# One head's product with adj on GpSimd in the attention stage of a graph-attention kernel

## The chip, the cores and the metric

The kernel runs on one core of a Trainium2 chip. A core has TensorE (PE), VectorE (DVE), ScalarE (ACT), GpSimd (POOL) and SyncE (SP), which issues most transfers here. The metric is the device time of one launch in microseconds, as the median of several runs. Before the change it is 981.29 us (3 runs, 978.91 to 981.9).

## The reference

One graph layer with three attention heads, then a mixture-of-experts layer, over N = 3327 nodes with 128 features. What matters here, for each head with weights W and vector a:

```python
hW = h @ W
hp = (adj > 0) @ hW;  hm = (adj < 0) @ hW
e_plus = leaky_relu(concat([hp, hm]) @ a, 0.2)      # one score per node
att = where(adj > 0, e_plus[None, :], NEG_INF)      # e_minus where adj < 0
att = softmax(att, axis=1)
edge_support += (att * adj) @ hW
```

The diagonal of adj is taken out first. Two GRU cells take the sums further, and the experts follow. In the data adj has no negative entries, so the "plain" branches of the kernel run; a flag made on the chip chooses them.

## The kernel before

N is padded to 3328: 26 tiles of 128 nodes (TILES) down the contracted axis, and 7 column chunks (CHUNKS), the first 256 wide and six 512 wide. The work has stages in a fixed order written out by hand, each engine with its own list of instructions, joined by semaphores. The change touches one stage, the attention over the tiles.

In it every score is used relative to its row's top: the weight of column node c and row node r is exp(shift - max(row[r] - score[c], 0)), and the denominators are multiplied in at the end. For chunk c and tile t (n = 26 c + t) these steps follow each other:

- DVE, `distance` (L1371): two tensor_scalar instructions, heads 0 and 1, subtract and maximum, into wexp slot n % 4 (SLOTS = 4). It counts g_y.
- ACT (L880): relu of head 2's distance into the same slot, counted by g_relu; then one exponential over heads 0 and 1 (L884) and one over head 2 (L886), which counts g_e.
- DVE, `product` (L1380): one tensor_tensor over all three heads, wexp slot times the tile of adj from the ring, the same tile for each head, into wadj buffer n % 2. It waits for g_e and for g_mm, with which TensorE gives the buffer back, and counts g_w.
- PE, `sum_heads` (L1906): one matmul for each head, h[t] times wadj, accumulated over the 26 tiles in three PSUM banks. Each is two records in the profile. The last counts g_mm.

DVE makes tile t + 1's distance ahead of tile t's product. `keep(c)` (L1322 to L1330) multiplies the three finished PSUM banks into `heads`, one instruction a head, eight tiles into the next chunk. The first chunk takes its rows from first_rows (shown as node_w), the others from rowbuf (shown as rows). The loops of DVE and ACT are hardware loops (Fori) with four tiles in a body; TensorE's part is written out.

The tiles of adj come through a ring of 18 slots in thirds of a chunk (THIRDS: tiles 0 to 7, 8 to 15, 16 to 25). SP's `load_third` issues the load of a third when the third two before it has been used (g_w), and puts other transfers behind it in its queue: zero fills of sorted_dram, the broadcasts of the rows (stats_dram, counted by k_in), and weights. POOL's only work in the stage is to clear the diagonal block of each tile that the diagonal crosses (`clear_diagonal`, an affine_select, L657), after each load and ahead of DVE; it counts g_clear, for which DVE waits before the first product of a third. In a later stage POOL makes three elementwise instructions per chunk for the first cell, `edge_mixed` (L692 to L694).

Of the kernel before, what the change touches and what calls it, by code (L numbers as in the profile page):

```python
# [26 lines left out]
H = 128  # L27
HEADS = 3
TILES = -(-N // 128)
# [7 lines left out]
SLOT = 8  # L37
ROWS = 3
SLOTS = 4
ALPHA = 0.2  # L40
# [65 lines left out]
class InOrder:  # L106


    def __init__(self, engine, semaphore):
        self.engine, self.semaphore, self.value = engine, semaphore, 0  # L110
# [26 lines left out]
def graph_layer_kernel(nc, x, x_t, adj_rows, adj_cols, diag, ident_in, sum_parts_in, level_at_in,  # L137
# [9 lines left out]
    with ctx:  # L147
# [216 lines left out]
        g_clear, g_relu, g_order_dve = (sem(f"g_{n}") for n in ("clear", "relu", "order_dve"))  # L364
# [101 lines left out]
        def _(sp):  # L466
# [174 lines left out]
        def _(pool):  # L641
# [10 lines left out]
            def clear_diagonal(c, t, tile):  # L652
# [10 lines left out]
            for c in range(NCH):  # L663
                for part, (t0, t1) in enumerate(LOADS):
                    pool.wait_ge(a_in[part] if c > 0 else a_first[part], 16 * max(c, 1))
                    if c == 0 and t1 > MAIN:
                        pool.wait_ge(a_in_tail, 16)
                    for t in range(t0, t1):
                        clear_diagonal(c, t, cols_of(c, t, t + 1).squeeze(1))
                    nc.gpsimd.nop().then_inc(a_clear, 1)  # L670

            for c in range(NCH):
                for third, (t0, t1) in enumerate(THIRDS):
                    at = (3 * c + third) % 2 * SLOT
                    pool.wait_ge(g_in[third], (32 if third == 2 else 16) * (c + 1))
                    for t in range(t0, t1):
                        clear_diagonal(c, t, ring[:, at + t - t0 if t < t0 + SLOT else SLOT + t - t0, :])
                    nc.gpsimd.nop().then_inc(g_clear, 1)  # L678
# [44 lines left out]
        def _(act):  # L723
# [131 lines left out]
            LAST = HEADS - 1  # L855

# [13 lines left out]
            def exponentials_plain():  # L870

                for c, (c0, w) in enumerate(CHUNKS):

                    def tile(t, k):

                        n = TILES * c
                        slot = (n + k) % SLOTS
                        place = wexp[:, slot, LAST, 0:w]
                        act.wait_ge(g_w, t + (n + 1))
                        nc.scalar.activation(place, row_of(c, LAST), ACT.Relu,  # L880
                                             bias=h[:, bass.ds(t, 1), H + SCORES + LAST]).then_inc(g_relu, 1)
                        act.wait_ge(g_y, t + (n + 1))
                        both = wexp[:, slot, 0:LAST, 0:w]
                        nc.scalar.activation(both, both, ACT.Exp, bias=shift[:, 0:1], scale=-1.0)  # L884
                        act.wait_ge(g_relu, t + (n + 1))
                        nc.scalar.activation(place, place, ACT.Exp, bias=shift[:, 0:1], scale=-1.0).then_inc(g_e, 1)  # L886

                    if c < len(k_in):
                        act.wait_ge(k_in[c], 16)
                    if c == 0:  # L890
                        tiles_by_four(act, 0, SLOT, tile)
                        keep_rows()
                        tiles_by_four(act, SLOT, TILES, tile)
                    else:
                        tiles_by_four(act, 0, TILES, tile)
# [137 lines left out]
        def _(dve):  # L1033
# [327 lines left out]
            def products_plain():  # L1361
# [3 lines left out]
                def distance(c, t, k):  # L1365

                    c0, w = CHUNKS[c]
                    n = TILES * c
                    dve.wait_ge(g_w, t + (n + 1))
                    for i in range(HEADS - 1):  # L1370
                        last = nc.vector.tensor_scalar(wexp[:, (n + k) % SLOTS, i, 0:w], row_of(c, i),  # L1371
                                                       h[:, bass.ds(t, 1), H + i], 0.0, ALU.subtract, ALU.max)
                    last.then_inc(g_y, 1)

                def product(c, t, k, place):
                    c0, w = CHUNKS[c]
                    n = TILES * c
                    dve.wait_ge(g_e, t + (n + 1))
                    dve.wait_ge(g_mm, t + (n + 1))
                    nc.vector.tensor_tensor(wadj[:, k % 2, :, 0:w], wexp[:, (n + k) % SLOTS, :, 0:w],  # L1380
                                            ring[:, bass.ds(place, 1), 0:w].broadcast_to([128, HEADS, w]),
                                            ALU.mult).then_inc(g_w, 1)

                dve.wait_ge(k_in[0], 16)
                distance(0, 0, 0)
                for c in range(NCH):
                    for first, end, at in stretches(c):
# [3 lines left out]
                        if end - first < SLOTS:  # L1391
                            for t in range(first, end):
                                if t + 1 < TILES:
                                    distance(c, t + 1, t + 1)
                                elif c + 1 < NCH:
                                    if c + 1 < len(k_in):
                                        dve.wait_ge(k_in[c + 1], 16)
                                    distance(c + 1, 0, 0)
                                product(c, t, t, at + t - first)
                            continue  # L1400
                        with dve.Fori(0, (end - first) // SLOTS) as p:
                            for k in range(SLOTS):
                                distance(c, SLOTS * p + (first + k + 1), k + 1)
                                product(c, SLOTS * p + (first + k), k, SLOTS * p + (at + k))
# [307 lines left out]
        def _(pe):  # L1712
# [178 lines left out]
            def sum_heads(v):  # L1891
                for c, (c0, w) in enumerate(CHUNKS):
# [311 lines left out]
```

## Time and profile before

| | |
|---|---|
| median of 3 runs | 981.29 us |
| profiled execution, its span | 1004.0 us |
| around the span | the page gives nothing more of that execution |
| attention stage, from the first to the last matmul of L1906 | 262.6 to 716.5 us |
| busy in the span | PE 901.2, DVE 694.9, ACT 628.8, POOL 148.5 us |
| L1906, 1092 matmul records | 444.0 us busy |
| L1380, the product | 299.1 us busy |
| L1371, the distances | 137.1 us busy in the 512 wide chunks |

The profiled execution is one launch taken by the hardware profiler. Its times are microseconds from the first instruction. Durations in groups are means of one instruction in nanoseconds. Matmuls overlap each other, so the distance between the starts of weight loads (PEld) says more about TensorE's pace than the duration of a matmul. Most instructions of DVE begin just before the one ahead has ended, so there too the distance of starts is the pace.

### The profile page before, as it was taken

How to read it: one execution, taken by the hardware profiler on the slowest of the kernel's cores; microseconds unless marked ns; L12 is line 12 of the kernel's file. 1: busy time of each engine (PE TensorE's matmuls, PEld its weight loads, DVE VectorE, ACT ScalarE, POOL GpSimd, SP SyncE). 2: the span in 40 equal slices, each digit the busy share in tenths (PEclk: the TensorE clock that was granted, in tenths of full speed). 3: DMA queues.
4: the chain of work that ended last, by engine and by line, in shares of the span. 5: the costliest groups of instructions: out<-in, count | busy, mean ns of one | idle time of the engine just before them, and what ended most of it. 6: DMA issues, size and time to landing. Idle time of an engine off the chain costs nothing.

```text
span 1004.0 us, 10398 instructions
## 1 busy us (share of the span) xinstructions
PE 901.2 (90%) x2770; PEld 458.4 (46%) x2770; DVE 694.9 (69%) x1287; ACT 628.8 (63%) x922; POOL 148.5 (15%) x184
## 2 busy tenths in 40 slices
PE   5999999899799999999999999999998771587787
PEld 5634343466674344444444444444544331376542
DVE  6523333352799899999999999999667785321234
ACT  2345554511799898998998989989433331564531
POOL 0000000000000000010000001010132555256540
PEclk9999999999899999999999999999999895699989
DMA  9877767220089956645445465220300021455523
GB/s 283 305 249 270 261 228 257 71 87 16 10 214 318 328 180 183 145 120 143 121 121 144 118 179 168 84 104 1 119 1 6 27 72 35 133 145 166 154 98 123
DMA packets 100635, 145.26 MB, mean 145 GB/s; under 512 B 11469, under 2 KB 51079, under 8 KB 99559
## 3 DMA queue, kind: packets, MB, share of 16 engines
q1 hardware_dynamic: 97318, 137.90, 45.5%
q0 software_dynamic: 3264, 6.74, 1.9%
q8 instruction: 24, 0.39, 0.2%
q14 instruction: 29, 0.23, 0.1%
HBM read 122.02 MB, written 22.60 MB: 144 GB/s over the span
## 4 chain that ended last, share of the span: by engine, by line
PE 46%; issue 24%; DVE 19%; ACT 4%; DVEq 3%; POOL 2%; another core or an unknown queue 1%; DMA 1%; SPq 0%; ACTq 0%; POOLq 0%
PE psum L1788 15%; DVE work L1371 9%; PE psum L1906 7%; PE psum L1872 4%; DVE big L1380 3%; PE psum L2093 3%; PE psum L2104 2%; PE psum L2063 2%; DVEq L1371 2%; PE psum L1944 1%; PE psum L1945 1%; PE psum L1771 1%; POOL sorted_dram L703 1%; PE psum L1949 1%; PE psum L1727 1%
## 5 line engine op out<-in xcount | busy, mean ns | idle before, releaser
L1906 PE MATMUL psum<-big,h 128*128 128x512 f32 (+1 forms) x1092 | 444.0, 568 | 13.2 <-DVE big L1380 13.0
L1906 PEld LDWEIGHTS psum<-big,h 128*128 128x128 f32 x1092 | 206.1, 191 | 250.2 <-issue 176.3
L1380 DVE TENSOR_TENSOR big<-work,big 128x1536 f32<-128x1536 f32 (+1 forms) x182 | 299.1, 1643 | 8.3 <-ACT work L886 2.5
L884 ACT ACTIVATE work<-work,shift 128x1024 f32<-128x1024 f32 (+1 forms) x182 | 198.3, 1089 | 42.2 <-DVE work L1371 38.9
L1788 PE MATMUL psum<-big,h 128*128 128x512 f32 x312 | 146.3, 611 | 0.0
L1371 DVE TENSOR_SCALAR work<-rows,h 128x512 f32<-128x512 f32 x312 | 137.1, 482 | 2.8 <-POOLq L678 2.8
L886 ACT ACTIVATE work<-work,shift 128x512 f32<-128x512 f32 (+1 forms) x182 | 123.4, 678 | 0.0
L657 POOL TENSOR_SCALAR_AFFINE_SELECT big<-big 128x128 f32<-128x128 f32 x50 | 25.2, 505 | 633.7 <-DMA big<-adj_cols_dram 631.5
L880 ACT ACTIVATE work<-rows,h 128x512 f32<-128x512 f32 x156 | 110.6, 709 | 0.0
L1788 PEld LDWEIGHTS psum<-big,h 128*128 128x128 f32 x312 | 56.6, 191 | 68.9 <-issue 68.4
L756 ACT ACTIVATE work<-big 128x2048 bf16<-128x2048 f32 (+1 forms) x42 | 75.0, 1786 | 11.9 <-POOLq L670 9.3
L1126 DVE TENSOR_SCALAR rows<-big 128x2048 fp8e4<-128x2048 f32 x36 | 42.5, 1224 | 48.9 <-POOLq L670 48.7
L1672 DVE TENSOR_SCALAR rows<-psum,rows 128x128 f32<-128x128 f32 x58 | 17.7, 348 | 76.2 <-PE psum L2114 30.1
L716 POOL DMA_INDIRECT y_dram<-rows x58 | 55.6, 959 | 54.3 <-DVE rows L1663 37.6
L703 POOL DMA_INDIRECT sorted_dram<-big x44 | 43.9, 997 | 33.1 <-issue 12.5
L1113 DVE TENSOR_TENSOR work<-work,psum 32x512 f32<-32x512 f32 (+1 forms) x7 | 4.5, 637 | 54.2 <-ACT work L771 54.2
L2093 PE MATMUL psum<-work,rows 128*128 128x256 f32 x116 | 32.5, 406 | 7.3 <-ACT work L996 5.1
L2104 PE MATMUL psum<-work,rows 128*128 128x256 f32 x116 | 32.4, 404 | 5.7 <-issue 3.4
L1872 PE MATMUL psum<-rows,work 128*126 128x512 fp8e4 (+1 forms) x168 | 35.0, 364 | 0.0
L1005 ACT ACTIVATE work<-psum,rows 128x256 f32<-128x256 f32 x58 | 24.5, 479 | 15.3 <-PE psum L2093 11.4
L771 ACT ACTIVATE work<-psum 32x512 f32<-32x512 f32 (+1 forms) x7 | 3.9, 557 | 39.1 <-PE psum L1749 39.0
L2104 PEld LDWEIGHTS psum<-work,rows 128*128 128x128 f32 x116 | 22.9, 202 | 11.2 <-issue 4.7
(296 smaller groups left out, 832.8 us busy)
## 6 DMA issues: line engine op xcount, KB each, us to landing
big<-adj_cols_dram SPq DMA_DIRECT2D x30, 2048.0 KB, 8.0
sorted_dram<-zeros SPq DMA_DIRECT2D x15, 910.0 KB, 14.3
big<-adj_cols_dram SPq DMA_DIRECT2D x9, 1024.0 KB, 7.3
big<-adj_cols_dram SPq DMA_DIRECT2D x6, 1536.0 KB, 6.5
rows<-experts_dram SPq DMA_DIRECT2D x29, 257.5 KB
rows<-stats_dram SPq DMA_DIRECT2D x1, 4608.0 KB, 27.2
rows<-stats_dram SPq DMA_DIRECT2D x1, 3840.0 KB, 20.4
rows<-sorted_dram SPq DMA_DIRECT2D x29, 130.0 KB
```

The source lines that it names most:

```text
L716: nc.gpsimd.indirect_dma_start(out=y_dram[:, :], out_offset=bass.IndirectOffsetOnAxis(ap=where_i[:, n, k:k + 1], axis=0), in_=y_sb[:, n % ...
L756: nc.scalar.activation(unused[:, 0:t1 - t0, 0:w], cols_of(c, t0, t1), ACT.Relu, scale=-1.0, accum_out=negative[:, NQ * c + g:NQ * c + g + ...
L880: nc.scalar.activation(place, row_of(c, LAST), ACT.Relu, bias=h[:, bass.ds(t, 1), H + SCORES + LAST]).then_inc(g_relu, 1)
L884: nc.scalar.activation(both, both, ACT.Exp, bias=shift[:, 0:1], scale=-1.0)
L886: nc.scalar.activation(place, place, ACT.Exp, bias=shift[:, 0:1], scale=-1.0).then_inc(g_e, 1)
L1371: last = nc.vector.tensor_scalar(wexp[:, (n + k) % SLOTS, i, 0:w], row_of(c, i), h[:, bass.ds(t, 1), H + i], 0.0, ALU.subtract, ALU.max)
L1380: nc.vector.tensor_tensor(wadj[:, k % 2, :, 0:w], wexp[:, (n + k) % SLOTS, :, 0:w], ring[:, bass.ds(place, 1), 0:w].broadcast_to([128, HEA ...
L1788: last = nc.tensor.matmul(bank[2 + c % 2][:, 0:w], h[:, t, 0:H], cols_of(c, t, t + 1).squeeze(1), start=t == 0, stop=t == TILES - 1)
L1872: last = nc.tensor.matmul(bank[6 + c % 2][0:STAT * LH, 0:w], weights[k][:, t - PREP * k, 0:STAT * LH], mask_of(t, c), start=t == 0, stop=t ...
L1906: done = nc.tensor.matmul(sums[i], h[:, t, 0:H], wadj[:, t % 2 if v == "plain" else 0, i, 0:w], start=t == 0, stop=t == TILES - 1)
L2093: last = nc.tensor.matmul(bank[2 + n % 2][:, a * BATCH:(a + 1) * BATCH], w1_of[a][:, n % NX, :], turned[:, n % 3, :], start=True, stop=True)
L2104: last = nc.tensor.matmul(bank[4 + n % 2][:, 0:BATCH], w2_of[a][:, n % NX, :], act_h[:, n % 3, a, :], start=a == 0, stop=a == HALVES - 1)
```

## The change

DVE's product covers heads 0 and 1 (1024 elements wide instead of 1536); POOL makes head 2's with a tensor_tensor of its own and counts g_p. PE, ACT's relu and SP's loads get a wait on g_p. ACT's relu is issued a tile ahead, and one exponential covers all three heads. DVE makes the distances two tiles ahead. POOL clears the diagonal of the next third after tiles 3, 11 and 20 of a chunk, between products, where it had no order with products before. The loops of DVE and ACT are written out. LAST is 2, the third head.

```diff
 (SP, load_third)
                     sp.wait_ge(used, TILES * ((n - 2) // 3) + THIRDS[(n - 2) % 3][1] + credit)
+                    sp.wait_ge(g_p, TILES * ((n - 2) // 3) + THIRDS[(n - 2) % 3][1])
 (POOL)
+            def clear_third(order, n):
+
+                c, third = n // 3, n % 3
+                t0, t1 = THIRDS[third]
+                at = n % 2 * SLOT
+                pool.wait_ge(g_in[third], (32 if third == 2 else 16) * (c + 1))
+                for t in range(t0, t1):
+                    clear_diagonal(order, c, t, ring[:, at + t - t0 if t < t0 + SLOT else SLOT + t - t0, :])
+                nc.gpsimd.nop().then_inc(g_clear, 1)
+
+            def products():
+
+                clear_third(plain_order, 0)
+                for c, (c0, w) in enumerate(CHUNKS):
+                    for t in range(TILES):
+                        n = TILES * c + t
...
+                        pool.wait_ge(g_e, n + 1)
+                        pool.wait_ge(g_mm, n + 1)
+                        nc.gpsimd.tensor_tensor(wadj[:, n % 2, LAST, 0:w], wexp[:, n % SLOTS, LAST, 0:w], ring[:, at, 0:w],
+                                                ALU.mult).then_inc(g_p, 1)
+                        if t in (3, 11, 20) and 3 * c + t // 8 + 1 < 3 * NCH:
+                            clear_third(plain_order, 3 * c + t // 8 + 1)
 (ACT, exponentials_plain)
+                def distance(c, t):
...
+                    if n >= SLOTS:
+                        act.wait_ge(g_p, n - SLOTS + 1)
+                    nc.scalar.activation(wexp[:, n % SLOTS, LAST, 0:w], row_of(c, LAST), ACT.Relu,
+                                         bias=h[:, t:t + 1, H + SCORES + LAST]).then_inc(g_relu, 1)
+
+                distance(0, 0)
                 for c, (c0, w) in enumerate(CHUNKS):
...
+                        act.wait_ge(g_y, n + 1)
+                        act.wait_ge(g_relu, n + 1)
+                        place = wexp[:, n % SLOTS, :, 0:w]
                         nc.scalar.activation(place, place, ACT.Exp, bias=shift[:, 0:1], scale=-1.0).then_inc(g_e, 1)
 (DVE, products_plain)
+                def product(c, t, place):
...
+                    nc.vector.tensor_tensor(wadj[:, n % 2, 0:LAST, 0:w], wexp[:, n % SLOTS, 0:LAST, 0:w],
+                                            ring[:, place:place + 1, 0:w].broadcast_to([128, LAST, w]),
                                             ALU.mult).then_inc(g_w, 1)
...
-                distance(0, 0, 0)
+                distance(0, 0)
+                distance(0, 1)
...
+                        for t in range(first, end):
+                            ahead = TILES * c + t + 2
+                            if ahead < TILES * NCH:
+                                distance(ahead // TILES, ahead % TILES)
+                            product(c, t, at + t - first)
 (PE, sum_heads)
                         pe.wait_ge(g_w, TILES * c + t + 1 + SLOTS)
+                        if v == "plain":
+                            pe.wait_ge(g_p, TILES * c + t + 1)
```

## Rows read from the trace of the kernel before

**Rows 1.** The page: busy time, share of the span and instructions of each engine.

```profile
PE 901.2 (90%) x2770; PEld 458.4 (46%) x2770; DVE 694.9 (69%) x1287; ACT 628.8 (63%) x922; POOL 148.5 (15%) x184
```

**Rows 2.** Busy time by stretch: PE, PEld, DVE, ACT, POOL; then clock, DMA share, GB/s.

```profile
439.50:507.90 68.40, 67.25 (x157) 29.47 (x156) 67.75 (x82) 61.91 (x79) 2.76 (x4) 1.00 0.54 141
```

**Rows 3.** Timeline of DVE, 512 wide chunk: start, us, engine, line.

```profile
480.45 1.76 DVE L1380 TENSOR_TENSOR big<-work,big 128x1536 f32<-128x1536 f32 x1
482.13 0.88 DVE L1371 TENSOR_SCALAR work<-rows,h 128x512 f32<-128x512 f32 x2
483.03 1.76 DVE L1380 TENSOR_TENSOR big<-work,big 128x1536 f32<-128x1536 f32 x1
```

**Rows 4.** Timeline of the weight loads at the end of the stage.

```profile
713.28 0.19 PEld L1906 LDWEIGHTS psum<-big,h 128*128 128x128 f32 x1 [0.24 <-DVE big L1380]
...
715.85 0.19 PEld L1949 LDWEIGHTS psum<-support,big 128*128 128x128 f32 x1 [0.24 <-issue]
```

**Rows 5.** Timeline of SP's queue: the same third of two chunks.

```profile
439.50 0.37 SPq L510 DMA_DIRECT2D big<-adj_cols_dram  x1
...
507.87 0.37 SPq L510 DMA_DIRECT2D big<-adj_cols_dram  x1
```

**Rows 6.** Groups of the span by form: count, busy us, mean ns, idle before.

```profile
L1380 DVE TENSOR_TENSOR big<-work,big 128x1536 f32<-128x1536 f32 x156 | 274.2, 1758 | 5.0 <-issue 1.1 <-PE psum L1906 0.8 <-ACT work L886 0.3
L1380 DVE TENSOR_TENSOR big<-work,big 128x768 f32<-128x768 f32 x26 | 24.9, 956 | 3.3 <-ACT work L886 2.2 <-PE psum L1906 1.1
L1329 DVE TENSOR_TENSOR rows<-rows,psum 128x512 f32<-128x512 f32 x18 | 11.3, 680 | 3.3 <-PE psum L1906 3.3
```

**Rows 7.** Timeline of DVE, first chunk.

```profile
271.13 0.95 DVE L1380 TENSOR_TENSOR big<-work,big 128x768 f32<-128x768 f32 x1
...
272.53 0.95 DVE L1380 TENSOR_TENSOR big<-work,big 128x768 f32<-128x768 f32 x1
```

**Rows 8.** Groups of POOL by form, later stage.

```profile
L694 POOL TENSOR_TENSOR work<-work 128x512 f32<-128x512 f32 x5 | 6.3, 1262 | 0.4
L694 POOL TENSOR_TENSOR work<-work 128x256 f32<-128x256 f32 x1 | 0.7, 725 | 0.1
```

**Rows 9.** Timeline of DVE and POOL, later stage.

```profile
788.31 0.69 DVE L1446 TENSOR_TENSOR work<-work 128x512 f32<-128x512 f32 x1
789.04 1.94 DVE L1447 TENSOR_TENSOR work<-work 128x512 f32<-128x512 f32 x1
789.13 1.28 POOL L692 TENSOR_TENSOR work<-h_t,work 128x512 f32<-128x512 f32 x1
...
790.50 1.61 POOL L693 TENSOR_TENSOR work<-work 128x512 f32<-128x512 f32 x1
```

**Rows 10.** Timeline of DVE and POOL, later stage, small operands.

```profile
760.38 0.21 DVE L1507 TENSOR_TENSOR big<-big 128x48 f32<-128x48 f32 x1
...
766.31 1.27 POOL L693 TENSOR_TENSOR work<-work 128x512 f32<-128x512 f32 x1
766.44 1.20 DVE L1573 TENSOR_TENSOR big<-big 128x48 f32<-128x48 f32 x1
```

**Rows 11.** Timeline, attention stage: a diagonal clearing and a distance.

```profile
450.12 0.36 POOL L657 TENSOR_SCALAR_AFFINE_SELECT big<-big 128x128 f32<-128x128 f32 x1
...
450.25 0.51 DVE L1371 TENSOR_SCALAR work<-rows,h 128x512 f32<-128x512 f32 x1
```

**Rows 12.** DMA issues at 301.17, 321.83 and 439.50: size, us to landing.

```profile
big<-adj_cols_dram SPq DMA_DIRECT2D x1, 2048.0 KB, 18.9
...
big<-adj_cols_dram SPq DMA_DIRECT2D x1, 2048.0 KB, 20.9
...
big<-adj_cols_dram SPq DMA_DIRECT2D x1, 2048.0 KB, 8.4
```

**Rows 13.** PE's busy time by stretch, with the granted clock behind it.

```profile
870.00:880.00 10.00, 8.13 (x43) 1.00 0.29 79
...
910.00:920.00 10.00, 8.23 (x36) 0.83 0.55 158
```

More of the change, by code:

```diff
@@ L39 @@
 SLOTS = 4
+LAST = HEADS - 1
 ALPHA = 0.2
@@ L363, in graph_layer_kernel @@
         g_y, g_e, g_w, g_mm, g_kept = (sem(f"g_{n}") for n in ("y", "e", "w", "mm", "kept"))
-        g_clear, g_relu, g_order_dve = (sem(f"g_{n}") for n in ("clear", "relu", "order_dve"))
+        g_clear, g_relu, g_order_dve, g_p = (sem(f"g_{n}") for n in ("clear", "relu", "order_dve", "p"))
         early_in, t_ready = sem("early_in"), sem("t_ready")
@@ L650, in _, with clear_diagonal @@
                 .then_inc(consts, 1)
-            def clear_diagonal(c, t, tile):
+            def clear_diagonal(order, c, t, tile):
                 c0, w = CHUNKS[c]
@@ L668, in _ @@
                     for t in range(t0, t1):
-                        clear_diagonal(c, t, cols_of(c, t, t + 1).squeeze(1))
+                        clear_diagonal(order, c, t, cols_of(c, t, t + 1).squeeze(1))
                     nc.gpsimd.nop().then_inc(a_clear, 1)
[L672 to L678, printed above, removed]
+            def clear_third(order, n):
[6 more added lines that the diff above has]
+                nc.gpsimd.nop().then_inc(g_clear, 1)
@@ L679, in _ @@
+            plain_order, signed_order = (InOrder(pool, pool_order, order.value) for _ in range(2))
+            pool.wait_ge(f_ready, 1)
+            signed = pool.value_load(flag[0:1, 0:1])
+            with pool.If(signed > 0):
+                nc.gpsimd.nop().then_inc(g_p, TILES * NCH)
+                for n in range(3 * NCH):
+                    clear_third(signed_order, n)
+            with pool.Else():
+                products()
+            order.value = plain_order.value
             pool.wait_ge(sorted_clear, 16 * PARTS)
@@ new lines, in distance @@
+                def distance(c, t):
+                    w = CHUNKS[c][1]
+                    n = TILES * c + t
+                    if t == 0 and c < len(k_in):
+                        act.wait_ge(k_in[c], 16)
+                    if n >= SLOTS:
+                        act.wait_ge(g_p, n - SLOTS + 1)
+                    nc.scalar.activation(wexp[:, n % SLOTS, LAST, 0:w], row_of(c, LAST), ACT.Relu,
+                                         bias=h[:, t:t + 1, H + SCORES + LAST]).then_inc(g_relu, 1)
@@ new lines, in exponentials_plain @@
+                distance(0, 0)
+                for c, (c0, w) in enumerate(CHUNKS):
+                    for t in range(TILES):
+                        n = TILES * c + t
+                        if t + 1 < TILES:
+                            distance(c, t + 1)
+                        elif c + 1 < NCH:
+                            distance(c + 1, 0)
+                        act.wait_ge(g_y, n + 1)
+                        act.wait_ge(g_relu, n + 1)
+                        place = wexp[:, n % SLOTS, :, 0:w]
+                        nc.scalar.activation(place, place, ACT.Exp, bias=shift[:, 0:1], scale=-1.0).then_inc(g_e, 1)
+                        if c == 0 and t == SLOT - 1:
+                            keep_rows()
@@ L1363, in products_plain, with distance @@
                 nc.vector.nop().then_inc(g_w, SLOTS)
[L1365 to L1372, printed above, removed]
-                    last.then_inc(g_y, 1)
[L1375 to L1381, printed above, removed]
+                def distance(c, t):
+                    w = CHUNKS[c][1]
+                    n = TILES * c + t
+                    if t == 0 and c < len(k_in):
+                        dve.wait_ge(k_in[c], 16)
+                    dve.wait_ge(g_w, n + 1)
+                    for i in range(LAST):
+                        last = nc.vector.tensor_scalar(wexp[:, n % SLOTS, i, 0:w], row_of(c, i),
+                                                       h[:, t:t + 1, H + i], 0.0, ALU.subtract, ALU.max)
+                    last.then_inc(g_y, 1)
+                def product(c, t, place):
+                    w = CHUNKS[c][1]
+                    n = TILES * c + t
+                    dve.wait_ge(g_e, n + 1)
+                    dve.wait_ge(g_mm, n + 1)
+                    nc.vector.tensor_tensor(wadj[:, n % 2, 0:LAST, 0:w], wexp[:, n % SLOTS, 0:LAST, 0:w],
+                                            ring[:, place:place + 1, 0:w].broadcast_to([128, LAST, w]),
                                             ALU.mult).then_inc(g_w, 1)
-                dve.wait_ge(k_in[0], 16)
-                distance(0, 0, 0)
+                distance(0, 0)
+                distance(0, 1)
                 for c in range(NCH):
@@ L1390, in products_plain @@
                         dve.wait_ge(g_clear, 3 * c + min(first // SLOT, 2) + 1)
[L1391 to L1404, printed above, removed]
+                        for t in range(first, end):
[3 more added lines that the diff above has]
+                            product(c, t, at + t - first)
                 keep(NCH - 1)
```

26 lines of the change are left out of this document (4 added, 22 removed).

## The prediction, made before the changed kernel was run

> **What bounds the kernel now.** I read the busy shares first [rows 1]: TensorE 90%, VectorE 69%, and GpSimd only 15%, so GpSimd looks like free room. Shares of a span mix stages, so next comes the table by stretch [rows 2]. It shows one column chunk of 26 tiles in the middle of the attention stage, 68.4 us, with PE busy 67.3, DVE 67.8 and ACT 61.9 us of it. Two engines are full at once. The rows of one tile say how full [rows 3]. DVE starts a tile's product at 480.45 and the next at 483.03, 2.57 us apart: the product's successor starts 1.67 us after it (482.13), and the two distances take 0.88, 0.02 from the next start. That is 1.67 + 0.90 = 2.57 with no gap. TensorE, at the end of the stage when all data lie ready, starts its weight loads 0.43 us apart, the six of a tile from 713.28 to 715.85 [rows 4]: also 2.57 us, and the granted clock of the stretch is 1.00 [rows 2]. So DVE and TensorE tie, and any relief of DVE alone is worth nothing inside a tile. What it can give back lies in two places. First, SyncE issues the load of the same third of two successive chunks at 439.50 and 507.87 [rows 5]: 68.37 us per chunk, 1.45 more than 26 x 2.57 = 66.9. That is DVE's keep() between two chunks, three instructions of 0.68 us [rows 6], partly covered. Second, in the first chunk, of half width, DVE's products start 1.40 us apart [rows 7], against 2.57 / 2 = 1.29 for TensorE.
>
> **The change, step by step.** *(1) DVE's product shrinks from 1536 to 1024 elements.* The 1536 and 768 element forms take 1.758 and 0.956 us [rows 6]: 1.044 ns an element, so 512 fewer are 0.53 us. DVE's own tile falls to 2.57 - 0.53 = 2.04 us, and in the first chunk to 1.40 - 0.27 = 1.13.
>
> *(2) ACT.* It is busy 61.9 / 26 = 2.38 us per tile [rows 2] and does the same elements in one instruction fewer, so it stays below the other bounds: worth nothing. The relu moved a tile ahead and the distances moved two tiles ahead take latency out of a chain that holds nobody up now. ACT's relu gets a new wait, for GpSimd's product of four tiles before; behind it stands the exponential of the present tile, but four slots are over 9 us of cover against a product that may take 2.4.
>
> *(3) GpSimd's new product of 512 elements.* The same operation, type and size stands in a later stage: 1.26 us, and 0.73 for 256 [rows 8]. Against 2.57 us a tile it seems to fit easily, and by engine busy times alone the change would be free. But look at what DVE does while such a product runs [rows 9]. DVE's L1447 (two SBUF inputs, 512 elements) takes 1.94 us where the same form one instruction earlier took 0.69. It started at 789.04; GpSimd's L692 ran 789.13 to 790.41; DVE ended 790.98, 0.57 after GpSimd, and its 512 elements need 0.53. So DVE moved nothing until GpSimd was through. The reverse stands there too: GpSimd's next product, started 790.50, took 1.61, and ended 1.13 after DVE's end at 790.98. A second place [rows 10]: a DVE product of 48 elements takes 1.20 us, ending 767.64, with a GpSimd product ending 767.58; its form costs 0.21 [the first of rows 10]. And the distances (one SBUF tensor in) are held as well [rows 11]: with GpSimd's diagonal clearing from 450.12 to 450.48, the distance started 450.25 ends 450.76, which is 450.48 plus 0.28. Its 512 elements take about that if they pass two at a time (0.53 / 2 = 0.27), and its free time is 0.44, half of rows 3's 0.88.
>
> So GpSimd's product and all three DVE instructions of a tile exclude each other, and their times add. What GpSimd adds to DVE's tile: it holds DVE off for 1.13 us, DVE starts some 0.03 after, and DVE's normal step between two instructions (1.67 less 1.60 of elements, 0.07) is covered: 1.13 + 0.03 - 0.07 = 1.09. Where it falls into the wider step between two distances (0.44 less 0.27 of elements = 0.17) it adds 0.99. I take 1.05: **2.04 + 1.05 = 3.09 us per tile**, against 2.57. Bounds: from below, elements alone at GpSimd's slope ((1.262 - 0.725) / 256 = 2.1 ns, so 1.07) with 1.07 and 0.53 of DVE, 2.67, some 2.8 with the steps between them; from above, DVE's measured loss in rows 9, 1.94 - 0.69 = 1.25, so 3.3.
>
> The Trainium skill (SBUF — State Buffer, "Who interferes with whom") calls this an exclusive lock: a DVE instruction with two SBUF inputs, or in a two-port mode, and a GpSimd instruction that reads SBUF block each other for the whole instruction. Rows 9 to 11 agree on who blocks whom. Taken to the letter, with GpSimd's whole 1.26 us added to 2.04, a tile would be 3.30 us and the time 156 x 0.21 = 33 us above my forecast; by rows 9 a part of it (1.26 - 1.13) hides behind the instruction before.
>
> The sum: a chunk is 26 x 3.09 = 80.3 us plus 1.5 for keep(), which reads PSUM for its second input and may let GpSimd's product pass beside it: 81.8, or +13.5 over 68.37. Six chunks: **+81 us**. First chunk: GpSimd's 256 elements add 1.05 - (1.26 - 0.73) = 0.52, so 1.13 + 0.52 = 1.65 against 1.40, 26 times: **+6**. TensorE's 2.57 fits into 3.09, and with two wadj buffers a buffer is back after both products (2.4 in sequence), the matmuls (2.57) and waits of some 0.3: 5.3 us, within two tiles' 6.2. So the buffer loop doesn't bind.
>
> *(4) GpSimd's diagonal clearing now stands in line with products.* clear_third waits for the load of the next third after tiles 3, 11 and 20; behind it is the next tile's product, then TensorE. The load is issued when its ring slots come free, 4 or 5 tiles earlier, 12.4 to 15.5 us at the new pace. In the steady stage 2 MB land in 8.4 us: no cost. Two early ones took 18.9 (issued 301.17) and 20.9 us (321.83) [rows 12], crowded by the broadcasts of stats_dram and the zero fills; until now they were needed 8 tiles after. Now GpSimd would stand 18.9 - 12.4 = 6.5 and 20.9 - 12.4 = 8.5 us; the slower pace thins the crowd, and DVE runs ahead meanwhile, so about half: **+7** (bounds 0 and 15). SyncE's new wait for g_p delays a load by GpSimd's lag, under a tile, and stands before the same zero fills and early weight loads; the slack is above. DVE's wait for k_in comes a tile earlier, with two tiles' products queued behind it; the broadcasts go out before the loads of rows 12, and these are in before the chunk that reads them.
>
> *(5) Loops written out.* Nothing: TensorE's part is already written out and its loads keep their 0.43 pitch [rows 4]; DVE's steps show no loop gap in rows 3 to be won. If code came late, it would show as idle before it; I allow 0 to +5.
>
> Together 81 + 6 + 7 = **+94 us**. The profiled execution's span is 1004.0 us; with it the sum gives 1098. The page has no time around the span, and the median of the runs is 981.29, 22.7 below. The stage runs at full clock with PE and DVE at their own pitch, so nothing in it is stretched by profiling, and I add the +94 to the median: 981.3 + 94 = 1075, and with half a microsecond each for GpSimd's new branch and the stage's last product **1076 us**.
>
> **The rivals.** *No exclusion (the change works).* For it: GpSimd idles 85% of the span, and rows 9 to 11 are few instructions, most on other tiles. Then TensorE binds: a chunk falls to 66.9 (6 x 1.45 = 9 us), the first gives 26 x 0.11 = 3: 969 us. Against it: every overlapped pair in the groups shows the block, in both directions. It turns at one point: GpSimd's product must add less than 0.53 us to DVE's tile, what it takes off; above that the kernel is slower. 5%.
>
> *Partial overlap.* The products alternate so that steps and start-ups hide: 2.8 us per tile, 156 x 0.23 = 36, and 2 each for the first chunk and the loads: +40, 1021 us. Nothing in the rows speaks for it but that the samples are few. 10%.
>
> *Worse: TensorE's clock falls.* At 2.57 of 3.09 us TensorE is 83% busy in bursts. A later stretch with 82% busy shows a granted clock of 0.83 [rows 13], another with 81% one of 1.00. A clock of 0.83 is a third of the time at 1.2 GHz, where a tile takes 5.14: of 480 us, 160 make 31 tiles instead of 52, 21 x 3.09 = 65 us more: 1141 us. Against it: the gaps are 0.5 us, and those of the later stage are longer. 13%, with a GpSimd that queues up behind loads for the full 16 us in the same class.
>
> **How the numbers follow.** Forecast 72%, the rivals 5, 10 and 13. About 0.3% (3 us) is what can be told from no change. Faster: 5%, the first rival. Of the partial case's 10, 2 may land within 0.3%; the rest is slower, 72 + 8 + 13 = 93%. Range: 156 tiles at 2.9 with no load waits give 51 + 4 = +55, 1036; at 3.3 with the load waits 114 + 8 + 12 = +134, 1115. 1040 to 1114 leaves out some 10% on either side.
>
> **What would show it.** In the changed profile GpSimd's product should take over 1.3 us on average, up to 2.3, although free it takes 1.27; where DVE's distances are 0.88 for two now, one of them should often pass 1.3, or its 1024 form the 1.76 - 0.53 = 1.22 that it costs free; the same third's load should be issued some 82 us apart; PE should wait about half a microsecond per tile, ended by whichever product came last. GpSimd should stand on a DMA after tiles 3 and 11 of the second chunk only. I am wrong if DVE's forms keep their free times while GpSimd's product runs, or if chunks are below 75 us; and wrong in size if the clock row leaves 1.00.

## The result, and the profile after

The changed kernel takes 1039.57 us (median of 4 runs, 1037.46 to 1041.93) against 981.19: a ratio of 1.0597, 95% interval 1.0581 to 1.0613. It is 58.4 us slower. The forecast was 94 us slower, 1076, with a range of 1040 to 1114: the side and the mechanism came out, the size was too large by 36 us and the time lies just under the range. One execution of a later run, half_product, took 1148.7 us at a granted clock of 0.79 and is left out of its time.

The page of the changed kernel shows what a busy share hides. The row that answers to [rows 1]:

```profile
PE 935.0 (90%) x2770; PEld 446.4 (43%) x2770; DVE 756.0 (73%) x1287; ACT 598.2 (58%) x740; POOL 398.2 (38%) x366
```

GpSimd took over a third of DVE's product, and DVE's busy time rose by 61 us. The groups by form of the attention stage say where [rows 6]; columns are count, busy us, mean ns, idle before:

```profile
L1402 DVE TENSOR_SCALAR work<-rows,h 128x512 f32<-128x512 f32 x312 | 278.9, 934 | 0.0
L694 POOL TENSOR_TENSOR big<-work,big 128x512 f32<-128x512 f32 x156 | 230.1, 1476 | 225.5 <-PE psum L1931 213.1 <-DMA big<-adj_cols_dram 6.5 <-ACT work L922 5.1
L1412 DVE TENSOR_TENSOR big<-work,big 128x1024 f32<-128x1024 f32 x156 | 197.3, 1265 | 8.3 <-PE psum L1931 8.2
```

The product shrank as worked out (1.22 free, 1.27 on average). But the distances, which the change hardly touches, went from 137.1 us in 312 instructions to 278.9. The timelines of DVE and of GpSimd show one tile; each row is taken from a stretch that cuts the pair of distances apart, since a merged row would hide which of the two is held:

```profile
603.52 1.21 DVE L1412 TENSOR_TENSOR big<-work,big 128x1024 f32<-128x1024 f32 x1
604.66 0.47 DVE L1402 TENSOR_SCALAR work<-rows,h 128x512 f32<-128x512 f32 x1
...
605.05 1.49 DVE L1402 TENSOR_SCALAR work<-rows,h 128x512 f32<-128x512 f32 x1
606.47 1.21 DVE L1412 TENSOR_TENSOR big<-work,big 128x1024 f32<-128x1024 f32 x1
```

```profile
604.83 1.43 POOL L694 TENSOR_TENSOR big<-work,big 128x512 f32<-128x512 f32 x1 [1.52 <-PE psum L1931]
```

GpSimd starts its product at 604.83, when TensorE gives the buffer back, and waits until the first distance ends (604.66 + 0.47 = 605.13). It is through at 606.26, 1.13 us later, the hold read in [rows 9]. The second distance starts at 605.05 and ends at 606.54, 0.28 after GpSimd. So a tile is 1.14 (product to first distance) + 0.39 (first to second distance) + 1.42 (second distance to next product) = 2.95 us, where TensorE needs 2.57 (the median over chunks 3 to 6 is 2.944). The chain of waits of that stretch, in order of time (start, us, what), has nothing else in it; the 1.49 of L1402 is the held distance:

```profile
602.11 1.49 DVE work L1402
603.60 1.13 DVE big L1412
604.73 0.01 DVE work L1402
604.75 0.30 issue
605.05 1.49 DVE work L1402
```

By stretch, the columns as in [rows 2], DVE is never idle and TensorE's rows cover 95% at full clock, though it needs only 2.57 of 2.95 us. SyncE issues the same third 77.59 us apart, where [rows 5] had 68.37:

```profile
470.10:547.70 77.60, 73.76 (x156) 27.49 (x156) 77.60 (x82) 56.89 (x53) 40.01 (x30) 1.00 0.50 124
```

```profile
437.68 0.37 SPq L512 DMA_DIRECT2D big<-adj_cols_dram  x1
...
515.27 0.37 SPq L512 DMA_DIRECT2D big<-adj_cols_dram  x1
```

From the first weight load of each chunk to that of the next, the seven chunks took 41.5, 69.8, 68.4, 68.4, 68.4, 68.5 and 68.2 us before (453.3 in all) and 48.3, 81.8, 77.5, 77.6, 77.7, 77.6 and 76.4 after (516.9). That is 63.6 more; what lies ahead of the stage is the same to 0.2 us.

The profiled span of before (1004.0) can't be set against that of after (1037.4). The kernel before took 981 us on two of the chips used and 1004 and 1007 on two others. What follows the stage took 258 to 260 us in all profiles on the first kind, 282 to 288 on the second; it is 288.1 in the profile of before, so that one is taken to be of the second kind. So times are compared only with the runs of before on the same chip, and chunks, which don't differ by chip from the third on, across all.

### The profile page after: what moved, and what is told of

Same layout as the page of the kernel before. It is cut to its first block, busy times and chain, and to the rows that moved or that the text cites. A ratio compares the mean times of both kernels' runs of the same rounds, so it can differ in the third digit from the quotient of the medians.

```text
span 1037.4 us, 9741 instructions
## 1 busy us (share of the span) xinstructions
PE 935.0 (90%) x2770; PEld 446.4 (43%) x2770; DVE 756.0 (73%) x1287; ACT 598.2 (58%) x740; POOL 398.2 (38%) x366
## 4 chain that ended last, share of the span: by engine, by line
DVE 46%; PE 33%; issue 8%; DMA 5%; POOL 4%; ACT 2%; SPq 2%; DVEq 0%; POOLq 0%; PEld 0%; ACTq 0%
DVE work L1402 21%; DVE big L1412 17%; PE psum L1811 15%; DMA big<-adj_cols_dram 4%; PE psum L1895 4%; PE psum L1931 2%; PE psum L2088 2%; POOL y_dram L746 2%; PE psum L1794 1%; POOL sorted_dram L733 1%; PE psum L1750 1%; PE psum L2165 1%; PE psum L1969 1%; PE psum L1970 1%; PE psum L1974 1%
## 5 line engine op out<-in xcount | busy, mean ns | idle before, releaser
L1931 PE MATMUL psum<-big,h 128*128 128x512 f32 (+1 forms) x1092 | 486.8, 584 | 34.3 <-POOL big L694 12.1
L694 POOL TENSOR_TENSOR big<-work,big 128x512 f32<-128x512 f32 (+1 forms) x182 | 251.8, 1385 | 290.1 <-PE psum L1931 233.9
L922 ACT ACTIVATE work<-work,shift 128x1536 f32<-128x1536 f32 (+1 forms) x182 | 269.9, 1483 | 121.5 <-DVE work L1402 121.4
L1931 PEld LDWEIGHTS psum<-big,h 128*128 128x128 f32 x1092 | 196.6, 193 | 323.7 <-issue 174.0
L1402 DVE TENSOR_SCALAR work<-rows,h 128x512 f32<-128x512 f32 x312 | 278.9, 934 | 0.0
L1412 DVE TENSOR_TENSOR big<-work,big 128x1024 f32<-128x1024 f32 (+1 forms) x182 | 216.1, 1187 | 13.4 <-PE psum L1931 13.2
L1811 PEld LDWEIGHTS psum<-big,h 128*128 128x128 f32 x312 | 56.6, 192 | 68.7 <-issue 68.0
L2118 PE MATMUL psum<-work,rows 128*128 128x256 f32 x116 | 29.9, 381 | 1.9 <-ACT work L1025 1.9
L2129 PE MATMUL psum<-work,rows 128*128 128x256 f32 x116 | 30.0, 381 | 0.0
L1895 PEld LDWEIGHTS psum<-rows,work 128*126 128x126 bf16 x168 | 21.9, 136 | 11.1 <-issue 0.5
```

What stands on the lines that cost most here:

```text
L694: nc.gpsimd.tensor_tensor(wadj[:, n % 2, LAST, 0:w], wexp[:, n % SLOTS, LAST, 0:w], ring[:, at, 0:w], ALU.mult).then_inc(g_p, 1)
L1402: last = nc.vector.tensor_scalar(wexp[:, n % SLOTS, i, 0:w], row_of(c, i), h[:, t:t + 1, H + i], 0.0, ALU.subtract, ALU.max)
L1412: nc.vector.tensor_tensor(wadj[:, n % 2, 0:LAST, 0:w], wexp[:, n % SLOTS, 0:LAST, 0:w], ring[:, place:place + 1, 0:w].broadcast_to([128, L ...
L1811: last = nc.tensor.matmul(bank[2 + c % 2][:, 0:w], h[:, t, 0:H], cols_of(c, t, t + 1).squeeze(1), start=t == 0, stop=t == TILES - 1)
L1895: last = nc.tensor.matmul(bank[6 + c % 2][0:STAT * LH, 0:w], weights[k][:, t - PREP * k, 0:STAT * LH], mask_of(t, c), start=t == 0, stop=t ...
L1931: done = nc.tensor.matmul(sums[i], h[:, t, 0:H], wadj[:, t % 2 if v == "plain" else 0, i, 0:w], start=t == 0, stop=t == TILES - 1)
```

## The experiments

Times are in us, "before" is the kernel before on the same chip. "Steady" are chunks 3 to 6, "second" is the second chunk, both from weight load to weight load. Before_again, before_third, three_quarters, product_twice, memset, extra_1, extra_3 and product_only are one execution each (and before is one for the last three), the others are medians of 4 to 10.

| run | time | before | steady | second |
|---|---|---|---|---|
| before_again | 1003.7 | 1003.6 | 68.4 | 71.6 |
| before_third | 1008.2 | 1007.5 | 68.4 | 75.4 |
| after_again | 1041.6 | 981.3 | 77.6 | 82.4 |
| no_product | 1001.3 | 1003.6 | 67.2 | 75.9 |
| dve_all | 1001.1 | 1003.6 | 68.2 | 69.9 |
| half_product | 1006.6 | 1003.6 | 67.4 to 68.1 | 77.0 |
| three_quarters | 1035.1 | 1007.5 | 71.9 to 72.5 | 79.3 |
| product_twice | 1241.0 | 1007.5 | 103.8 to 106.8 | 103.1 |
| memset | 981.0 | 981.3 | 67.2 | 80.0 |
| late_clear | 1031.6 | 981.3 | 77.0 to 77.7 | 77.0 |
| extra_1 | 980.6 | 981.0 | 68.2 to 68.7 | 72.4 |
| extra_3 | 997.3 | 981.0 | 71.3 to 72.5 | 71.1 |
| product_only | 1042.6 | 981.0 | 77.5 to 78.0 | 84.5 |
| spread_keep | 975.7 | 981.3 | 67.2 to 67.5 | 73.1 |
| late_fills | 992.8 | 1007.5 | 67.2 to 67.5 | 66.6 |

**Controls.** The kernels before and after once more.

> The kernel before once more, for a second profile. The stage after the attention took 287.5 us in the profiled execution of before and 257.3 in that of the changed kernel, although the median of before is 22.7 us below its profiled span. Theory 1: the long tail was that one execution's own (the expert batches), and a second profile shows a span near 980, the attention stage again 454 us and a tail of 262 to 266. Theory 2: the tail of before is really some 30 us longer under the profiler, and the change shortened it; then the span is near 1004 again.

> The changed kernel once more, on the chip of these runs, where the kernel before takes 1003.6 us and not 981. Its attention stage took 516.9 us against 453.3, 63.6 more, but the medians differ by 58.4 only. Theory 1: the stages after the attention last longer on this chip (283 to 288 us in all four profiles so far, 258 in the changed kernel's), whatever the kernel; then the difference here is about 60 to 66 us, 1064 to 1070, with a stage of 517 us and a tail above 275. Theory 2: the change itself shortens the tail by 5 us or more; then the tail is again near 258 and the time near 1040.

> The kernel before a third time. Where this run takes about 981 us, its profile gives the stages after the attention as they are on the chip on which the changed kernel was compared. If the change leaves them alone (theory 1), its tail is 258 to 260 us like the others there; the medians differ by 60.2 us where the attention stage differs by 63 to 65, so some 263 us would mean that the changed kernels win 3 or 4 us behind the stage (theory 2).

Before_again did not bring the short tail: it fell on a chip where before takes 1004, and before_third on one where it takes 1007. After_again fell on one where before takes 981, 60.2 us slower (ratio 1.062, 1.060 to 1.064) with a stage of 517.7. The long tail goes with the chip in every profile, whatever the kernel, though neither theory named this outcome rightly for before_again. The kernel before was never profiled on a chip of the 981 kind. Its second chunk alone ranges from 69.8 to 75.4 us, which covers the 3 to 5 us between 63.6 and the 58.4 and 60.2 of the medians; whether it is that was not shown.

**Is it GpSimd's product?** Leaving it out, and giving it back to DVE:

```diff
 no_product
-  nc.gpsimd.tensor_tensor(wadj[.., LAST, ..], wexp[.., LAST, ..], ring[:, at, 0:w], ALU.mult).then_inc(g_p, 1)
+  nc.gpsimd.nop().then_inc(g_p, 1)
 dve_all (and no wait on g_p anywhere; GpSimd clears in its own order)
-  nc.vector.tensor_tensor(wadj[:, n % 2, 0:LAST, 0:w], ..., [128, LAST, w] ...)
+  nc.vector.tensor_tensor(wadj[:, n % 2, :, 0:w], ..., [128, HEADS, w] ...)
```

> The changed kernel with GpSimd's product left out (head 2's sum is then not the reference's); its waits, its place in the queue and its count g_p stay. Theory A (GpSimd's product and DVE's instructions exclude each other, adding 1.0 us to DVE's tile of 1.93): DVE needs 1.93 us a tile, TensorE 2.57, so TensorE binds, chunks are 67 to 68 us, the attention stage about 438 us instead of 517.7, the time 958 to 968. Rival B (the new waits, the clearing in line or the written out loops carry a good part of the loss): chunks stay above 70 us and the time above 985.

> The changed kernel with head 2's product back in DVE's instruction (1536 elements) and GpSimd only clearing diagonals, in no order with products; one exponential over three heads, relu a tile ahead, distances two tiles ahead and written out loops stay. Theory A: DVE's tile is 1.67 + 0.80 = 2.47 us, just under TensorE's 2.57, so the chunk is again 68.3 us and the time within 4 us of before, 977 to 983. Rival B: the other parts cost, over 990.

Both settle the steady stage: without the product a chunk is 67.2 us, TensorE's floor, busy from end to end at full clock:

```profile
448.00:515.20 67.20, 67.20 (x158) 29.58 (x157) 54.18 (x82) 56.61 (x53) 2.34 (x4) 1.00 0.55 144
```

With three heads on DVE it is 68.2, as before. The written out loops, the single exponential and the order ahead cost nothing and bring 0.2 us a chunk (dve_all is at 0.9974 of before, 0.9952 to 0.9997). But the time of no_product missed its forecast: only 2.3 us under before, not 13 to 23. The stage took 453.5 us instead of 438, and the whole miss lies in its first two chunks, 41.8 and 75.9 us where TensorE needs some 33.6 (half of 67.2) and 67.2. At the faster pace GpSimd, clearing in line, stands even longer for the loads: TensorE waited 8.5 us for its counts there.

**How does the cost grow?** With half, three quarters and twice the product:

```diff
 half_product (three_quarters: 3 * w // 4)
+  half = w // 2
+  nc.gpsimd.tensor_tensor(wadj[.., LAST, 0:half], wexp[.., LAST, 0:half], ring[:, at, 0:half], ALU.mult).then_inc(g_p, 1)
 product_twice
+  for again in range(2):
+      last = nc.gpsimd.tensor_tensor(... the whole product ...)
+      if again == 0:
+          plain_order.done(last)
+  last.then_inc(g_p, 1)
```

> The changed kernel with GpSimd's product over half the columns only (the other half of head 2's weights is left out). Theory A: 256 elements hold DVE off for 1.01 - 0.54 = 0.47 us, DVE's tile is 2.40 us, under TensorE's 2.57: the loss is gone whole, chunks about 68 us, time 960 to 972, as with no product at all. Rival C (the loss grows in proportion to GpSimd's busy time, by contention or waits of TensorE for it): half the loss stays, chunks 72 to 73 us and some 1005 us.

> The changed kernel with GpSimd's product over three quarters of the columns (384 of 512; the rest of head 2's weights is left out). Theory A: each 128 columns are 0.27 us of hold, so the tile is 2.94 - 0.27 = 2.67 us, just over TensorE's 2.57, and a steady chunk 70.2 to 70.8 us against 77.6 for 512 columns and 67.4 to 68.1 for 256. A loss in proportion to the columns from TensorE's floor would give (77.6 + 67.8) / 2 = 72.7.

> The changed kernel with GpSimd's product of 512 columns made twice into the same place, the second after the first is complete. GpSimd's own need is then some 2.7 us of a tile of 2.94. If its time adds to DVE's (theory A), the tile grows by the second product's hold, 1.05 to 1.15, to 4.0 us or so: chunks of 104 to 107 us, 1041 + 156 x 1.1 + 26 x 0.6 = some 1220 to 1235 us. If DVE and GpSimd ran side by side and the changed kernel were slow for another reason, 2.7 would fit and the time would stay under 1060.

The steady chunk goes 67.2 (nothing), 67.4 to 68.1 (256 columns), 72.0 (384), 77.6 (512), 104.8 (twice 512). Half of the product is nearly free, the last quarter costs 5.6 us: a sum that shows only above TensorE's floor, not a share. The time of half_product missed its forecast as that of no_product did, 3.0 us above before instead of 9 to 21 below, again by its second chunk (77.0). Three_quarters came between the two figures expected and nearer to the proportional one: 72.0, where the sum said 70.2 to 70.8 and the share 72.7. By itself it would not decide between them; half_product, where a share would give 72 to 73, does. Most of the 0.06 us a tile above the sum stands in its rows: a product of 384 columns starts at 603.85, the distance ahead ends at 603.92 and GpSimd at 604.85, so it holds DVE off for 0.93 us here (0.91 as the median) and not 1.13 - 0.27 = 0.86. In product_twice the second copy adds 1.01 us to the tile (602.45 to 606.41 is 3.96); both distances are held now, 2.90 us for the two. The time is 233.5 us over before on its chip; the 1220 to 1235 expected, set against 981, are 239 to 254. A tile:

```profile
602.45 1.21 DVE L1416 TENSOR_TENSOR big<-work,big 128x1024 f32<-128x1024 f32 x1
603.59 2.90 DVE L1406 TENSOR_SCALAR work<-rows,h 128x512 f32<-128x512 f32 x2
...
606.41 1.21 DVE L1416 TENSOR_TENSOR big<-work,big 128x1024 f32<-128x1024 f32 x1
```

GpSimd's own need of 2.7 us would have fitted into 2.95. It does not run beside DVE.

**What is it that excludes?** A GpSimd instruction that writes but doesn't read:

```diff
-  nc.gpsimd.tensor_tensor(wadj[:, n % 2, LAST, 0:w], ...)
+  nc.gpsimd.memset(wadj[:, n % 2, LAST, 0:w], 0.0).then_inc(g_p, 1)
```

> The changed kernel with GpSimd's product replaced by a memset of the same 512 columns of wadj (head 2's sum is left out): it writes and reads nothing. If only the reading counts against DVE's two-input product, that product keeps its 1.21 us while a memset runs, and the distances, if they use both ports for writing as well, are still held, by what the memset needs. If any GpSimd instruction excludes any of DVE's, both forms are lengthened where they overlap. Either way DVE's tile stays near 1.93 plus less than 0.5, under TensorE's 2.57: about the time of no_product, within 6 us.

The timelines of GpSimd and of DVE:

```profile
601.20 0.52 POOL L694 MEMSET big<- 128x512 f32 x1 [2.05 <-PE psum L1930]
...
606.35 0.64 POOL L694 MEMSET big<- 128x512 f32 x1 [2.05 <-PE psum L1930]
```

```profile
601.19 1.23 DVE L1411 TENSOR_TENSOR big<-work,big 128x1024 f32<-128x1024 f32 x1 [0.56 <-PE psum L1930]
...
606.45 0.82 DVE L1401 TENSOR_SCALAR work<-rows,h 128x512 f32<-128x512 f32 x1
```

DVE's two-input product keeps its 1.2 us with a whole memset inside it. The one-input distance does not: begun at 606.45 it ends at 607.27, 0.28 after the memset (606.99), instead of after 0.47. The whole run says the same: the 162 products that a memset overlaps take 1.23 us at most, and the seven distances that begin inside a memset end 0.28 us after it. So GpSimd's reading excludes DVE's two-input product, and its writing is enough to exclude the distance, which moves its 512 elements in that 0.28 us where a product needs 0.53. The Trainium skill (SBUF — State Buffer, "Who interferes with whom") has both: a DVE instruction with two SBUF inputs contends with a GpSimd instruction that reads SBUF, not with one that only writes, and one in a two-port mode contends with GpSimd, for which it makes no such exception. The trace agrees with that rule. Memset's steady chunk is 67.2 us, as in no_product; in the first two chunks GpSimd waited 18.5 us for loads before its memsets, against 6.5 before its products in the changed kernel, and the second is 80.0.

**Was DVE full before?** My step said 2.57 us of DVE's own. Small instructions of 0.08 us behind each product of dve_all:

```diff
+  for part in range(1):        # extra_3: range(3)
+      nc.vector.tensor_scalar(bn[:, t, 2 * part:2 * part + 2], h[:, t, 0:2], 0.0, None, ALU.add)
```

> dve_all with one more small DVE instruction (2 columns, of the kind that elsewhere starts 0.08 us before the next) behind each product. Theory S (DVE needs 2.47 us of its own and waits 0.1 a tile for a wadj buffer, shown as busy): 2.55 is still under 2.57, the steady chunk stays at 68.2 or rises by less than 1 us, since DVE makes up for keep() more slowly. Rival (DVE's tile is 2.57 of its own, as I predicted): every tile grows by 0.08, the chunk by 2.1 to 70.3.

> The same with three small instructions, 0.24 us a tile. Theory S: 2.47 + 0.24 = 2.71, DVE now sets the pace: steady chunk 26 x 2.71 + 1 to 2 = 71.5 to 72.5. Rival: 2.57 + 0.24 = 2.81, chunk 74.5 to 75.

One leaves the chunk at 68.2 to 68.7; three bring 71.3 to 72.5. So DVE had some 0.1 us of room in a tile.

**Do the other parts matter while the product is on GpSimd?**

```diff
 product_only (DVE's distances one tile ahead, ACT's relu in its own tile)
-  act.activation(wexp[:, n % SLOTS, :, 0:w], Exp)
+  act.activation(wexp[:, n % SLOTS, 0:LAST, 0:w], Exp); act.activation(wexp[:, n % SLOTS, LAST, 0:w], Exp)
```

> The changed kernel with the other parts undone: ACT's relu in its own tile, two exponentials, DVE's distances one tile ahead; loops stay written out and GpSimd's product and clearing stay. Under the exclusion alone (theory A) DVE's sequence is the same, 1.93 + 1.01, and ACT's 2.47 fits into it: steady chunk 77.5 to 78, the same as with the changes. Rival: being two tiles ahead hides a wait of DVE for ACT or of GpSimd for ACT; then the chunk is longer, 80 us or more.

No: 77.5 to 78.0 a chunk against 77.6. In its second chunk, 84.5, it is 2.1 to 2.7 us behind. But the rhythm is another one, and it shows both terms of the sum alone. The timeline of DVE:

```profile
605.84 1.21 DVE L1410 TENSOR_TENSOR big<-work,big 128x1024 f32<-128x1024 f32 x1
606.97 0.87 DVE L1400 TENSOR_SCALAR work<-rows,h 128x512 f32<-128x512 f32 x2
607.76 1.21 DVE L1410 TENSOR_TENSOR big<-work,big 128x1024 f32<-128x1024 f32 x1
608.90 2.90 DVE L1400 TENSOR_SCALAR work<-rows,h 128x512 f32<-128x512 f32 x2
611.72 1.21 DVE L1410 TENSOR_TENSOR big<-work,big 128x1024 f32<-128x1024 f32 x1
```

A tile without any GpSimd product in it takes 1.92 us, the next one, with two, 3.96: again 1.0 for each.

**The clearing in line.**

```diff
-  if t in (3, 11, 20) and 3 * c + t // 8 + 1 < 3 * NCH:
+  if t in (6, 14, 23) and 3 * c + t // 8 + 1 < 3 * NCH:
```

> The changed kernel with GpSimd's diagonal clearing after tiles 6, 14 and 23 instead of 3, 11 and 20, so that a third's load has three more tiles to land. Theory A with the loads: the second chunk, 81.8 us, comes down to 78 to 79 and the first, 48.3, by 1 to 3 us, the others stay at 77.6; together 4 to 6 us less than the changed kernel. Rival: the wait for loads isn't what makes the first two chunks long (broadcasts or DVE's own wait do), then less than 1 us.

The second chunk fell from 82.4 to 77.0, the first from 48.6 to 46.2, and the time by 10.0 us to 1031.6 (1.0511 of before, 1.0488 to 1.0533). GpSimd's wait for loads in them is 2.8 us, 6.5 in the changed kernel. The gain is more than expected, and a part of the change that can be had back without touching the product.

**Versions that beat both.** If DVE has 0.1 us a tile, keep() should hide in it when it doesn't come in one block; and the second chunk waits for loads that compete with zero fills.

```diff
 spread_keep (on dve_all)
-  if c > 0 and first == SLOT: keep(c - 1)
+  if c > 0 and t in (8, 14, 20): keep(c - 1, (8, 14, 20).index(t))     # one head, behind the product of tile t
 late_fills (on spread_keep)
-  if n - 3 in range(PARTS): ... cleared[:, n - 3, :, :]
+  if n - 6 in range(PARTS): ... cleared[:, n - 6, :, :]
```

> All three heads on DVE as in dve_all, and keep() split: one head after each of tiles 8, 14 and 20 of the next chunk instead of three in a row before tile 8. If DVE has 0.1 us of slack in a tile (2.47 against 2.57), as the changed kernel's DVE steps say, one head's 0.65 us is made good in 6 tiles and the chunk falls from 68.2 to 67.2 or 67.4: 5 to 7 us less than dve_all. If DVE has no slack (my prediction's 2.57 of its own), the 2 us a chunk cost the same 1.3 wherever they stand and the time doesn't move.

> spread_keep with the fifteen zero fills of sorted_dram (910 KB each) sent behind the loads of thirds 6 to 20 instead of 3 to 17, so that they no longer compete with the broadcasts and loads of the second chunk. The second chunk, 73.1 us there against 67.2 for the others, has a wait of several us for a load. If the crowding is the cause it falls to 67 to 69, and the time to 970 to 972; if the broadcasts of stats_dram (8.4 MB) alone are the crowd, it stays above 71.

Spread_keep takes 975.7 us, 0.9939 of before (0.9915 to 0.9962). Its chunk is TensorE's floor of 67.2. The timeline of DVE shows the recovery: after one head of keep() at 564.56 the tiles follow each other every 2.46 us (565.95, 568.41, 570.87) until the lag is gone:

```profile
564.56 0.68 DVE L1353 TENSOR_TENSOR rows<-rows,psum 128x512 f32<-128x512 f32 x1
565.16 0.87 DVE L1397 TENSOR_SCALAR work<-rows,h 128x512 f32<-128x512 f32 x2
565.95 1.75 DVE L1407 TENSOR_TENSOR big<-work,big 128x1536 f32<-128x1536 f32 x1
567.62 0.87 DVE L1397 TENSOR_SCALAR work<-rows,h 128x512 f32<-128x512 f32 x2
568.41 1.75 DVE L1407 TENSOR_TENSOR big<-work,big 128x1536 f32<-128x1536 f32 x1
...
570.87 1.75 DVE L1407 TENSOR_TENSOR big<-work,big 128x1536 f32<-128x1536 f32 x1
```

Late_fills brings the second chunk to 66.6 and the time to 992.8 on a chip where before takes 1007.5: 0.9854 of it (0.9820 to 0.9887), the best of all. The 970 to 972 expected were for a chip where before takes 981, 9 to 11 us less; measured are 14.7 less. Its whole stage is 443.9 us against 453.3 to 458.5 before.

## Why the prediction was right in kind and wrong in size

*The mechanism* was right: GpSimd's product and DVE's three instructions exclude each other, their times add, and DVE with GpSimd sets the pace instead of TensorE. No_product, half_product, product_twice and memset show it.

*The step that failed* is the sum of the tile, "2.04 + 1.05 = 3.09". It came to 2.95, 0.15 too high, which over 156 tiles is 23 of the 36 us. The larger part of the error is the first term, "2.57 with no gap" less 0.53. I took the distance of starts as DVE's own work. It held a wait. The merged row of the pair (0.88, [rows 3]) hid it; cut apart, the second distance of that pair starts at 482.52, and the product, as in [rows 3], at 483.03:

```profile
482.52 0.48 DVE L1371 TENSOR_SCALAR work<-rows,h 128x512 f32<-128x512 f32 x1
```

From first to second distance are 0.39 us, from the second to the product 0.51, since that product waits for TensorE's buffer (g_mm). A free one starts before the distance ahead has ended; this one starts 0.03 after (482.52 + 0.48 = 483.00), so of 0.12 us of wait only that shows as idle. Free, the step is 0.39 as well: in spread_keep's recovery both steps take 0.79 (565.16 to 565.95). The profile of before had it too, behind keep(), where DVE lags and waits for nobody:

```profile
462.70 1.75 DVE L1380 TENSOR_TENSOR big<-work,big 128x1536 f32<-128x1536 f32 x1
464.37 0.88 DVE L1371 TENSOR_SCALAR work<-rows,h 128x512 f32<-128x512 f32 x2
465.16 1.75 DVE L1380 TENSOR_TENSOR big<-work,big 128x1536 f32<-128x1536 f32 x1
```

So DVE's own tile was 2.46, not 2.57, and the new one 1.93, not 2.04. The statement that DVE and TensorE tie was wrong by the same 0.1: TensorE alone bound the tile. The second term was 1.01 instead of 1.05: GpSimd is started by TensorE's release of the buffer, nearly always at the same place, between the two distances, where I had half of the cases. (My 0.44 for a free distance, half of the pair's row, was no free time either: its row is 0.48 and the next instruction starts 0.39 after it.)

*keep()*: I gave it 1.5 us a chunk; 77.6 - 26 x 2.944 leaves 1.1, some 3 us over six chunks. That GpSimd's product may pass beside it came out: the one from 491.01 takes 1.28 us during keep(), whose three instructions keep their 0.68. *First chunk*: +6 forecast; its tiles came to 1.62 us (1.65 forecast), the chunk to +6.8, with other waits in it, among them GpSimd's four clearings in line (2.55 us from 296.65). *Loads*: +7 forecast. Above a steady chunk the second took 4.2 us, against 1.4 in the profile of before, so they cost some 3; late_clear gives back more (8.3 on the stage, 10.0 on the time), a part of it waits that the kernel before has too. GpSimd stood after tile 3 of the second chunk for 6.5 us, as worked out (18.9 - 12.4), but by luck: the load, issued at 307.78, took 16.3 us, and GpSimd was there 10.3 us after the issue.

```profile
324.57 2.49 POOL L694 TENSOR_TENSOR big<-work,big 128x512 f32<-128x512 f32 x2 [6.47 <-DMA big<-adj_cols_dram]
```

The second stand on a DMA, after tile 11, did not come; chunk 2 before, too, has its own wait, 2.8 us of DVE ahead of tile 16 (at 345.79), which I counted as nothing. *Written out loops*: nothing, as forecast (dve_all). *The clock* stayed at 1.00 in the steady chunks (0.98 in the second).

Of the 36 us, then, 30 lie in the stage (63.6 instead of 94): 23 in the tile, 3 in keep(), some 4 in the loads. The other 5 lie between the stage and the medians and stay open, as the controls show.

*The rivals.* No exclusion is refuted. Partial overlap, 2.8 us a tile and 1021, lies 19 us from the measured time, nearer than my 1076, and got 10%; but what was missing was not overlap, since the hold is the 1.13 us of [rows 9] whole. The fall of TensorE's clock did not come. The rule of the Trainium skill (SBUF — State Buffer, "Who interferes with whom"), taken to the letter as a hold of GpSimd's whole 1.26 us, is not what the rows show: 1.13 of hold, 1.01 added.

## What to carry to other kernels

An idle GpSimd is not free room beside a busy DVE: add its hold to DVE's tile and compare the sum with whatever bounds the stage, for only what stands above that floor costs. An engine that looks full by the distance of its starts may hide a wait under the end of the row ahead; before building on it, cut merged rows apart and look for a stretch in which it catches up. A gap between blocks (here keep()) may be worth more than the busiest instruction: spreading it, with all of the product on DVE, won 0.6%, and with transfers moved out of a crowded stretch 1.5%, each against before on its own chip.

## What the runs showed of the hardware that was not expected

- A GpSimd memset of 512 columns (0.53 us) leaves DVE's two-input product alone (1.23 us) and holds its one-input distance until it ends (0.82 instead of 0.48).
- A GpSimd product of 512 columns and DVE's two-input keep(), whose second input lies in PSUM, pass beside each other: 1.28 us and 0.68 a row in all five chunks of the changed kernel's profile where they meet.
- The same kernel takes 981 us on some chips of this kind and 1004 to 1007 on others. The stages after the attention take 258 to 260 us in the profiles on the former and 282 to 288 on the latter, while the steady chunks don't differ; the kernel before itself has no profile on a 981 chip, and the cause is open.
